# Target one-hots of a graph kernel: one comparison for a batch of buckets in place of one for each bucket

## The reference

```
def prop(v):                                   # layer 1, called twice: on x and on its own result
    return segment_sum(w_hat[:, None] * v[src], dst, num_segments=n)
def _L3_gnn_ref(x, src, dst):                  # layer 3: mean of the sources' rows
    msg_sum = segment_sum(x[src], dst, num_segments=n)
    return msg_sum / maximum(deg, 1.0)[:, None]
h = maximum(_layernorm(x), 0.0); x = x + layer(h, ...)      # four times
```

## Time and profile before

| | |
|---|---|
| median of 3 runs | 8358.81 us |
| profiled execution, its own time | 8364.93 us |
| span from the first to the last instruction | 8363.1 us |
| mean granted TensorE clock | 0.614 |
| busy: PE, DVE, ACT, POOL | 64%, 57%, 31%, 64% |
| line 1760, 4214 instructions | 902.3 us busy (631.1 in tbuf, 271.2 in H) |
| line 690, 5568 indirect DMAs | 5377.3 us busy |

### The profile page before, as it was taken

The page is one execution under the profiler, slowest core; times in us unless marked ns, Lnnn a source line. Parts: engine busy times, 40 slices in busy tenths (PEclk is TensorE's granted clock), DMA queues, the critical chain, the costliest instruction groups (busy, mean ns, idle before and its releaser), DMA issues.

```text
span 8363.1 us, 145338 instructions
## 1 busy us (share of the span) xinstructions
PE 5338.8 (64%) x39187; PEld 4254.1 (51%) x39188; DVE 4727.0 (57%) x15433; ACT 2564.9 (31%) x8163; POOL 5380.2 (64%) x5577
## 2 busy tenths in 40 slices
PE   5333333333276777777777777777777777786666
PEld 2222222222255555655545554477777777775555
DVE  5555555565588888644444444344444444448885
ACT  4444444444322222233333333312111111123221
POOL 2777777777577777444444443177777777766775
PEclk9555555555567666655555555555555555558997
DMA  6000000000122222234444434422222222213332
GB/s 160 14 14 14 14 14 14 14 14 14 24 52 51 51 51 51 63 134 139 136 140 143 144 133 137 142 41 41 41 41 41 41 41 41 41 35 86 88 88 59
DMA packets 463911, 542.65 MB, mean 65 GB/s; under 512 B 219394, under 2 KB 373026, under 8 KB 463710
## 3 DMA queue, kind: packets, MB, share of 16 engines
q0 software_dynamic: 178288, 148.77, 11.3%
q1 hardware_dynamic: 228973, 178.17, 8.1%
q10 hardware_dynamic: 56448, 213.62, 6.4%
HBM read 293.47 MB, written 246.66 MB: 65 GB/s over the span
## 4 chain that ended last, share of the span: by engine, by line
POOL 41%; PE 22%; issue 19%; DVE 7%; DVEq 5%; ACTq 2%; ACT 2%; DMA 1%; POOLq 0%; SPq 0%
POOL arena L690 41%; PE ps_agg L1083 6%; PE ps_wide L1310 5%; PE ps_agg L1204 3%; PE ps_wide L1188 2%; DVE tbuf L1760 2%; DVEq L1800 2%; PE ps_t L1310 2%; DVE msg L1799 1%; ACTq L1013 1%; PE ps_wide L1191 1%; ACT tbuf L1008 1%; DMA arena<-table,ibuf 1%; DVEq L1525 1%; PE ps_z L1288 1%
## 5 line engine op out<-in xcount | busy, mean ns | idle before, releaser
L690 POOL DMA_INDIRECT arena<-table,ibuf x3328 | 3155.1, 948 | 1240.1 <-issue 1144.9
L690 POOL DMA_INDIRECT arena<-nodes,ibuf x2240 | 2222.4, 992 | 1638.7 <-DVEq L1538 789.2
L1083 PE MATMUL ps_agg<-mem_a,arena 128*32 128x80 f32 (+1 forms) x3904 | 524.0, 321 | 570.9 <-DVEq L1525 558.7
L1083 PE MATMUL ps_agg<-mem_b,arena 128*32 128x80 f32 (+1 forms) x3904 | 476.6, 301 | 504.0 <-DVEq L1525 464.8
L1083 PEld LDWEIGHTS ps_agg<-mem_a,arena 128*32 128x32 f32 (+1 forms) x3904 | 461.9, 164 | 629.2 <-DVEq L1525 577.4
L1083 PEld LDWEIGHTS ps_agg<-mem_b,arena 128*32 128x32 f32 (+1 forms) x3904 | 417.4, 152 | 561.4 <-DVEq L1525 492.3
L1760 DVE TENSOR_SCALAR tbuf<-iota,at_f 128x256 bf16<-128x256 bf16 x2940 | 631.1, 299 | 0.5 <-PE ps_t L1204 0.3
L813 ACT ACTIVATE tbuf<-O,tbuf 128x49 bf16<-128x49 bf16 x2176 | 586.4, 363 | 118.0 <-DVE H L1675 118.0
L1341 PE MATMUL ps_agg<-tbuf,msg 128*64 128x80 f32 x2496 | 373.6, 344 | 330.4 <-DVE msg L1967 330.4
L1310 PE MATMUL ps_wide<-w2f,ht 33*128 33x462 f32 (+2 forms) x1078 | 557.0, 785 | 30.2 <-ACT tbuf L1008 30.2
L955 ACT ACTIVATE att<-score 128x8 f32<-128x8 f32 x208 | 43.3, 208 | 1650.1 <-DVE score L1958 1650.1
(11 more groups left out here) (379 smaller groups left out, 11206.0 us busy)
## 6 DMA issues: line engine op xcount, KB each, us to landing
table<-tbuf ACTq DMA_DIRECT2D x294, 544.5 KB
idx_a<-lows_d SPq DMA_DIRECT2D x602, 192.0 KB
arena<-table,ibuf POOLq DMA_INDIRECT x3328, 2.5
table<-tbuf ACTq DMA_DIRECT2D x98, 495.0 KB
arena<-nodes,ibuf POOLq DMA_INDIRECT x2240, 2.9
table<-tbuf SPq DMA_DIRECT2D x25, 1024.0 KB, 4.3
idx_a<-lows_d SPq DMA_DIRECT2D x86, 224.0 KB
nodes<-O SPq DMA_DIRECT2D x7, 224.0 KB, 3.0
```

The lines of the kernel that those rows point to most:

```text
L690: nc.gpsimd.indirect_dma_start(out=INTO[s][:, k, c, 0:WIDTH[s]], out_offset=None, in_=TABLE[s], in_offset=bass.IndirectOffsetOnAxis(ap=ibu ...
L1083: last = nc.tensor.matmul(ps_agg[ROW0[s]:ROW0[s] + CHN[s], 0:WIN], narrow[:, k, c, 0:CHN[s]], onehots[b][:, c, :], start=(c == 0), stop=(c ...
```

## The change

The comparisons of a batch's targets become one `tensor_tensor`. Its first input is `iota2`, read again for each bucket (a step of 0 over the buckets); its second is the slice of `slot_at` that holds the batch's 6 or 7 places, each read 256 times (a step of 0 in the innermost dimension). Both are bf16 and both lie in SBUF, the output as before is bf16 in SBUF. `at_f` and `start_block` go. The slice of `slot_at` depends on the block, so its address comes from a register in every step, where before only `start_block` had such an address.

```
-        at_f = sb("at_f", [P, 2, NBK])
 ...
                     dve.wait_ge(s_sent, count(i, e, q, 1))
-                    for k in range(n):
-                        op = V.tensor_scalar(to_oh[s][q % 2][:, k, :], iota2[:, :], at_f[:, e % UNIT[s], b0 + k:b0 + k + 1], None, ALU.is_equal)
-                    return op
+                    at = slot_at[:, bass.ds(i * (UNIT[s] * NBK) + ((e + q // NBATCH) * NBK + b0), n)]
+                    return V.tensor_tensor(to_oh[s][q % 2][:, 0:n, :], iota2[:, :].unsqueeze(1).to_broadcast([P, n, W2]),
+                                           at.unsqueeze(2).to_broadcast([P, n, W2]), ALU.is_equal)
 ...
-                def start_block(i, e):
-                    V.tensor_copy(at_f[:, e % UNIT[s], :], slot_at[:, bass.ds(i * (UNIT[s] * NBK) + e * NBK, NBK)])
 ...
-                        if q == 0 and not first:
-                            start_block(i, f)
 ...
-                            if q == 4 and (e + 1 < UNIT[s] or not last):
-                                start_block(i, n + 1)
```

More of the change, by code:

```diff
@@ L1786, in pick_weighed @@
                     if first:
-                        start_block(i, f)
-                        dve.drain()
                         compare_sources(i, f, 0)
@@ L1834, in pick_turn @@
                         if first and e == 0:
-                            start_block(i, n)
-                            dve.drain()
                             compare_sources(i, n, 0)
```

## The result

The changed kernel takes 8781.88 us (median of 4 runs, 8780.01 to 8784.49) against 8361.67 us for the kernel before (4 runs): ratio 1.0501, 95% interval 1.0488 to 1.0513. It is 5% slower. The forecast was 8815 us. The profiled execution after took 8783.4 us, with a span of 8781.6 us.

The account below looks back on a forecast made before the run. DVE and POOL were taken to bound pass 1, POOL pass 4, PE pass 2. Terms of 205, 10 and 245 us make +460 on 8364.9, adjusted to the median and given as 8815 us; 8-in-10 range 8450 to 8920.

Parts of the forecast that it names:

- The rate: Line 1759: the new comparison takes 1.75 us for 1536 elements, 2.01 for 1792, adding 3.77 us a block.
- The hold: A comparison with both inputs in SBUF stops one POOL DMA per step until it ends, 1.01 us on average.
- Pass 1: POOL, already filling this pass, is held in 208 steps and bounds it: +205 us.
- Pass 4: POOL bounds this pass and is held in 272 steps, less 30 us of present loss: +245 us.
- 272 x 1.01: Pass 4's POOL wait: 272 steps, each catching one DMA for 1.01 us on average, 275 us.
- A: The forecast itself: comparison at one element a cycle and POOL held, 8815 us, own range 8680 to 8920; chance 0.69.
- Pass 2: PE bounds this pass; POOL's added time hides in its slot waits, leaving +10 us.
- DVE alone: DVE's longer comparisons without any wait of POOL: +52 us in pass 1, +10 in pass 2, +43 in pass 4.
- Rival E: PE's clock falls too, as longer steps idle PE in pass 4: some 80 us on top of A, 8900 us; chance 0.07.
- B: Comparison at one element a cycle, POOL not held: +105 us, 8465 us; chance 0.11.
- C: Comparison at two elements a cycle, about 0.95 us, POOL held 0.28 us a step: +95 us, 8455 us; chance 0.08.
- D: Line 1759 at two elements a cycle and no hold: 20 to 50 us faster, 8325 us; chance 0.05.

Follow-up runs that it names:

- unit-step run: Changed kernel with the row of numbers also as the comparison's second input, advancing one element instead of 0: 8351.28 us, ratio 0.9985 to the kernel before, on X.
- X: The chip of the main result, where the kernel before takes 8362 us; three follow-up experiments ran there.
- PSUM run: Changed kernel with the numbers 0 to 255 read from an f32 copy in PSUM in passes 1 and 4: 8498.6 us, ratio 1.0161 to the kernel before, on X.
- halves: Changed kernel with each comparison cut in two over half the buckets: ratios 0.9845 and 0.9829 to the kernel before, on Y.
- Y: Three further chips taken together, where the kernel before takes 10,711, 10,731 and 10,907 us; nine experiments ran there.
- one by one: Kernel before with a two-input comparison per bucket, a second input replacing the scalar: ratios 0.9915 and 0.9957 to the kernel before, on Y.

## Why the prediction was right, step by step

**The rate (right).** 1.75 and 2.01 us were forecast from the slope between lines 1670 and 1944; 1748 to 1751 and 2013 to 2015 ns were measured. The 3.77 us more a block is what the rows give. The unit-step run shows the cause, the step of 0.

**The hold (right in kind).** One DMA caught in every comparison of passes 1 and 4 (but one), ending 0.82 us behind it, is what the timeline shows. Moving one input to PSUM, at an unchanged rate, removes it. Its wait of 1.01 us, reckoned for a random catch, came out as 1.16 us in pass 1 and 0.82 us in pass 4.

**Pass 1 (205 us forecast, 203.6 measured).** The close match is partly luck: the mean wait was larger than 1.01 us. POOL's time per DMA rose by 268 ns, and 832 x 0.268 = 223 us, some 20 us more than the pass lost. 6.7 of these can have gone into POOL's slot waits; where the rest went isn't shown. Nor was the catch random here: 80 of the 160 caught DMAs start 0.2 to 0.3 us into the comparison.

**Pass 4 (245 us forecast, 208.5 measured): a size was off.** The term "272 x 1.01" should have been 272 x 0.82 = 223 us; less some 15 of the former loss this is the measured (1388 - 1021) ns x 567 = 208 us. (The forecast took 30 us off for line 1760; of pass 4's 43 us of waits before, some 19 stood behind runs of that line.) The two engines fell into step, as the forecast's own objection to A had it. In a plain step of pass 4, comparisons stand 2.33 us apart (8203.28 to 8205.61). A held DMA ends 0.82 us behind a comparison and the next starts 0.30 later, 1.11 us behind that end and so 0.5 us into the next comparison, since only 0.6 us of other DVE work lies between. It can wait at most some 1.1 us there, not 1.63. So it is with 137 of the 271 caught DMAs, which start 0.5 to 0.6 us in; 101 start 1.1 to 1.3 us in and wait 0.42 us. In pass 1, the steps are long enough for two or three free DMAs in between, and the catches spread more.

**Pass 2 (10 us forecast, 5.6 with pass 3).** Hidden under POOL's slot waits, as worked out. `start_block` and the register instruction can't be seen by themselves on X.

**DVE alone (52, 10 and 43 us forecast; 59.9, 8.0 and 68.5 measured in the PSUM run).** Pass 1 is near. Pass 4 is 25 us short: I had taken off 57 us of slack and 25 for an early end. With DVE busy 730 of 800 us, POOL now idle for slots 101 us and three PE lines with 24% of the chain there, this is a pass that three engines share. The granted clock there is 0.86 where it was 0.95:

```profile
7634.00:8434.00 800.00, 560.30 (x6040) 477.48 (x6040) 730.27 (x977) 181.89 (x338) 540.73 (x553) 0.86 0.34 79
```

How much of the 25 us is the clock, and how much is slack counted too high, wasn't separated.

**Rival E (clock).** Its condition half came in: in pass 4 after the change the clock fell from 0.95 to 0.81 and PE's busy time rose from 496 to 609 us. But PE is not on that pass's chain, and the time lies at or under A's sum, so the fall cost nothing that can be seen beside POOL.

**Rivals B, C and D.** B's 8465 us stands against the PSUM run's 8499, 34 us too low by the DVE terms. C had a comparison of 0.95 us with the hold, at 8455 us (its own terms, 53 and 46, make 99 and not 95); the unit-step run took 8351, for it had priced a catch at 0.28 us a step where 0.06 (pass 1) and 0.11 us (pass 4) were measured. A random phase was the wrong picture there too: POOL's rhythm fell so that most DMAs that start in a comparison do so when it is nearly over. That run thus came near D, two elements a cycle and no hold, 8325 us.

## What to carry to other kernels

Before short one-input instructions are joined into one with two broadcast inputs, look at the inner step of both: here a step of 0 doubled its time, so the join put 688 comparisons in place of 4214 and still added 324 us of DVE. Then look at who starts work while the long instruction runs: with both inputs in SBUF here it held POOL's indirect DMAs, which cost twice as much as the slower rate, and one input in PSUM took that away at no cost in length. A wait between two engines with fixed rhythms is not random, so a mean over random phases is a rough guide: it missed by a fifth for the long comparison (1.16 and 0.82 us for 1.01), and was 2.6 and 5 times too high for the short one. Last, look in the trace whether an edit reached the instruction that it was meant for, above all when the time doesn't move.

## What was unexpected

- The hold is not bound to one instruction: a DMA waited through two halves (2.36 us instead of 0.94) and through the rest of seven short comparisons (2.37 us). The Trainium skill ("SBUF — State Buffer", two separate sides) describes a lock held for the whole of one instruction; these rows show that the change from one such instruction to the next need not let POOL in. When it does and when not stays open: pass 4 and pass 2 of the halves differ, with the same two instructions.
- A comparison with one f32 input in PSUM and a 16-bit one in SBUF took the same 1750 ns as with two 16-bit inputs in SBUF. With a step of 0 nothing of the rate was lost by it here.
- A two-input comparison of 256 elements takes 418 ns, the one-input form 278 to 299.
- On Y the order of the versions was another: halves 0.983 and 0.985, unit step 0.986, one by one 0.992 and 0.996, PSUM 0.995, all ahead of the kernel before; only the scalars straight from `slot_at` are behind it (1.015). The changed kernel itself wasn't run there. What the engines wait for there isn't in the profile, so why is open; and a choice between such versions made on one chip need not hold on another.
